# One list of expert tiles for both batches, in two parts, and the outputs summed one tile in every slot

## The reference

```python
x = x + xattn(layernorm(x), ctx, ctx, mask, W_out)       # 16 heads of 32, 128 keys
x = x + ffn(layernorm(x), proj_w, anchors, temp, w1, w2)
# ffn: logits from tanh(x @ proj_w.T / 0.3) against six anchor vectors;
# the two best of 6 experts by softmax of their two logits;
# h = gelu(x @ w1[e])   (512 -> 256);  y = h @ w2[e]   (256 -> 512)
# out = sum over the two chosen experts of weight * y
```

## Time and profile before

| | |
|---|---|
| median of 3 runs | 720.03 us (714.55 to 720.48) |
| the profiled execution | 721.91 us |
| its span, first to last instruction | 720.2 us |
| PE busy | 617.0 us (86%) |
| DVE, ACT, POOL busy | 451.5, 341.8, 301.0 us |
| mean granted TensorE clock | 0.918 |
| DMA | 126.25 MB, mean 175 GB/s |

### The profile page before, as it was taken

The page is one execution under the profiler, slowest core; times in us unless marked ns, Lnnn a source line. Parts: engine busy times, 40 slices in busy tenths (PEclk is TensorE's granted clock), DMA queues, the critical chain, the costliest instruction groups (busy, mean ns, idle before and its releaser), DMA issues.

```text
span 720.2 us, 15169 instructions
## 1 busy us (share of the span) xinstructions
PE 617.0 (86%) x4628; PEld 467.8 (65%) x4629; DVE 451.5 (63%) x968; ACT 341.8 (47%) x646; POOL 301.0 (42%) x434
## 2 busy tenths in 40 slices
PE   5989999999999999988788999999999999996000
PEld 4765566666656656444568898998999888885000
DVE  4846756665685866444986555684555676666455
ACT  4536855666847655574844554433333333331000
POOL 5423755555456656557671314130002233222774
PEclk9759999999999999899987999999999999999555
DMA  5301213222212373347372656485787788886787
GB/s 187 93 30 46 88 63 101 76 87 75 88 59 101 108 271 129 133 172 263 132 263 88 208 174 239 149 273 203 263 293 244 256 268 285 295 277 220 226 246 243
DMA packets 62577, 126.25 MB, mean 175 GB/s; under 512 B 7974, under 2 KB 11046, under 8 KB 62508
## 3 DMA queue, kind: packets, MB, share of 16 engines
q1 hardware_dynamic: 52268, 91.80, 37.7%
q0 software_dynamic: 10240, 33.56, 14.5%
HBM read 69.24 MB, written 56.10 MB: 174 GB/s over the span
## 4 chain that ended last, share of the span: by engine, by line
PE 55%; DVE 14%; issue 11%; DMA 7%; POOL 5%; SPq 3%; ACT 2%; DVEq 1%; POOLq 0%; ACTq 0%
PE ps L1477 7%; DMA y_d<-ysb 5%; PE ps L1499 4%; PE ps L1635 4%; PE ps L1522 3%; PE ps L1687 3%; PE ps L1524 3%; PE ps L1688 3%; PE ps L1523 3%; PE ps L1689 3%; PE ps L1711 3%; PE ps L1713 3%; PE ps L1673 3%; PE ps L1712 3%; PE ps L1590 3%
## 5 line engine op out<-in xcount | busy, mean ns | idle before, releaser
L802 POOL DMA_INDIRECT yg<-y_d,sidx x64 | 64.1, 1002 | 170.4 <-DVE wst L1320 133.9
L1078 DVE TENSOR_REDUCE nmax<-ps 128x4 f32<-128x512 f32 x128 | 82.3, 686 | 45.6 <-PE ps L1477 45.4
L917 ACT ACTIVATE prob<-ps 128x512 f32<-128x512 f32 x128 | 66.1, 603 | 84.2 <-PE ps L1502 81.4
L729 POOL DMA_INDIRECT xs_d<-x,place_now x64 | 67.2, 1049 | 81.0 <-PE ps L1689 66.8
L1687 PE MATMUL ps<-w1H,xgH 128*128 x296 | 90.5, 306 | 2.9 <-DVE xgL L1344 2.9
L1688 PE MATMUL ps<-w1H,xgL 128*128 x296 | 83.9, 283 | 0.0
L1689 PE MATMUL ps<-w1L,xgH 128*128 x296 | 83.8, 283 | 0.0
L996 ACT ACTIVATE xgH<-ps 128x512 fp32r<-128x512 f32 x74 | 44.2, 597 | 80.9 <-PE ps L1673 68.7
L1477 PEld LDWEIGHTS ps<-kfT,qT 32*128 32x128 f32 x1024 | 69.6, 202 | 18.9 <-issue 16.3
L1477 PE MATMUL ps<-kfT,qT 32*128 32x128 f32 x1024 | 76.9, 295 | 1.9 <-DVE nmax L1078 1.4
L1357 DVE COPY ysb<-ps 128x512 f32<-128x512 f32 x74 | 51.0, 689 | 31.4 <-PE ps L1713 19.6
(11 more groups left out here) (195 smaller groups left out, 1373.2 us busy)
## 6 DMA issues: line engine op xcount, KB each, us to landing
xg<-xs_d SPq DMA_DIRECT2D x74, 256.0 KB
y_d<-ysb SPq DMA_DIRECT2D x74, 256.0 KB
xin<-in_x SPq DMA_DIRECT2D x32, 256.0 KB, 2.7
x<-in_x SPq DMA_DIRECT2D x32, 256.0 KB
x_d<-x SPq DMA_DIRECT2D x32, 256.0 KB
x2t<-x_d SPq DMA_DIRECT2D x16, 256.0 KB, 4.1
x2c<-x_d SPq DMA_DIRECT2D x16, 256.0 KB, 4.7
out_x<-x2c SPq DMA_DIRECT2D x16, 256.0 KB
```

What stands on the lines that cost most here:

```text
L729: nc.gpsimd.indirect_dma_start(xs_d, bass.IndirectOffsetOnAxis(ap=place_now[:, n % 2, k, t:t + 1], axis=0), x2[:, n % 4, t, :], None).then ...
L802: nc.gpsimd.indirect_dma_start(yg[:, k, z, :], None, y_d[b], bass.IndirectOffsetOnAxis(ap=sidx[:, k, z:z + 1], axis=0))\
L917: nc.scalar.activation(prob[v % 2][:, h, :], ps[:, B_SC + h, :], ACT.Exp, scale=scale).then_inc(exp_done, 1)
L1078: nc.vector.tensor_reduce(nmax[:, n % 2, :, g * hpg + h], ps[:, token_bank(v, h), :].rearrange("p (t k) -> p t k", t=4), axis=AX.X, op=ALU ...
```

## The change

The expert regions hold both batches: region e has room for 4096 rows, and tokens of blocks 0 to 7 are placed one behind the other. There is one sequence of 69 tiles, the most that 8192 rows over 6 experts can need. The first 27 (T1) are full tiles of the rows of blocks 0 to 3 (4096 rows fill at least 27), so they need no zeros; the other 42 are ordered by the blocks after which a tile is full: those that blocks 0 to 3 fill first, then those that block 4 fills, and so on (`tiles_of_classes`, `first_of_classes`). So the results of blocks 0 to 3 are all in the first 37 tiles, those of block 4 in 45, of block 5 in 53, of block 6 in 61, of block 7 in 69 (`TILES_OF`).

Each list is made with one entry in each partition (`list_of`, ten small operations) and turned to a row by two PE transposes (`turn_list`), which DVE copies to the tables (`keep_list`). For the first list PE does this in the last but one attention step, and it waits for the copies before the projection of block 7, because bank 0 is used by both. For the second list PE waits in slot 23 until DVE is done with `list_of`, which it does at the end of its slot 22.

Token tile c is summed in slot 46 + c for c = 0 to 27, one in every slot, fetched by POOL two slots earlier; tiles 28 to 31 are done behind the loop. Residuals 0 to 15 are loaded in slots 28 to 43, the others five slots behind the sum whose buffer they take. From tile 26 on ACT copies the result to `ysb`. DVE's sums read `share` directly, without the small copies to `wst` and `sidx`. `SPAN` is 7, all loops are written out, and there is one `fill_up`, in slot 21.

```diff
-    NT = (2 * seq + EXPERTS * (P - 1)) // P
...
+    region = batches * seq + P
+    rows = EXPERTS * region
+    def most_tiles(n):
+        return (2 * n * blk + EXPERTS * (P - 1)) // P
+    T1 = 2 * NB1 * blk // P - (EXPERTS - 1)
+    tiles = most_tiles(nblk)
+    TILES_OF = [most_tiles(max(n + 1, NB1)) for n in range(nblk)]
...
-        SPAN = 8
+        SPAN = 7
...
-        TABLE = SPAN * LATE - 1
+        TABLE = SPAN * (LATE - 1) + 5
...
+        ONE_Y, BY_ACT = 20, 26
+        def expert_loop(body):
+            for i in range(n_iter):
                 body(i)
...
+        def put_slot(c):
+            s = TILES_OF[0] + 9 + c
+            return s if s < SLOTS and TILES_OF[c // 4] < tiles else None
...
@@ sync @@
-                if s == S_END - 1:
-                    fill_up(0)
...
+                    if TPI * i + k == TABLE + 2:
+                        fill_up()
...
+                        if w == T1:
+                            scattered_all(nblk)
+                            sp.wait_ge(pad_zero, 16 * EXPERTS)
...
+                    c = TPI * i + k - T1 - 1
+                    if live(c, RX):
+                        load_residual(c)
+                    for c in puts(TPI * i + k - 2):
+                        store_out(c)
+                    for c in puts(TPI * i + k - 5):
+                        if c + RX < ntok:
+                            load_residual(c + RX)
...
@@ gpsimd @@
+            def fetch_outputs(c):
+                pool.wait_ge(yrow_done, c // 4 + 1)
+                after(pool, cmb_done, c - RY + 1)
                 for z in range(2):
+                    nc.gpsimd.indirect_dma_start(yg[:, c % RY, z, :], None, y_d[0:TILES_OF[c // 4] * P, :],
+                                                 bass.IndirectOffsetOnAxis(ap=y_row[:, c, z:z + 1], axis=0))\
+                        .then_inc(yg_in[c % RY], 16)
...
+                    for c in puts(TPI * i + k + 2):
+                        pool.wait_ge(zp_ready, nblk)
+                        pool.wait_ge(up_ready, min(TPI * i + k - L_UP + 1, tiles))
+                        landed(c)
+                        fetch_outputs(c)
...
@@ scalar @@
+                    w, p, n = tl(i, k, L_DN)
+                    if live(w, tiles) and w >= BY_ACT:
+                        act.wait_ge(y_ready, w + 1)
+                        after(act, y_out[p], 16 * n)
+                        nc.scalar.activation(ysb[:, p, :], ps[:, y_bank(w, p), :], ACT.Copy).then_inc(ya_done, 1)
...
@@ vector @@
+            def put_together(c):
+                x = x2t[:, c % RX, :]
+                dve.wait_ge(x2t_in[c % RD], 16 * (c // RD + 1))
+                dve.wait_ge(yg_in[c % RY], 32 * (c // RY + 1))
+                nc.vector.scalar_tensor_tensor(x, yg[:, c % RY, 0, :], share[:, c, 0:1], x, ALU.mult, ALU.add).then_inc(half_done, 1)
+                dve.wait_ge(half_done, c + 1)
+                nc.vector.scalar_tensor_tensor(x, yg[:, c % RY, 1, :], share[:, c, 1:2], x, ALU.mult, ALU.add).then_inc(cmb_done, 1)
...
+                    if TPI * i + k == TABLE:
+                        tiles_of_classes()
+                    if TPI * i + k == TABLE + 2:
+                        first_of_classes()
+                    if TPI * i + k == TABLE + 3:
+                        list_of(CLASSES, nblk)
                         dve.wait_ge(share_done, nblk)
+                    if TPI * i + k == TABLE + 4:
+                        keep_list(B_LATE, T1, T2)
+                        rows_to_tiles()
+                    rows_of_tokens(TPI * i + k - TABLE - 5)
+                    for c in puts(TPI * i + k):
+                        put_together(c)
...
@@ tensor @@
+            def turn_list(bank, count):
+                pe.wait_ge(lst_done, count)
+                for z in range(2):
+                    last = nc.tensor.transpose(ps[0:1, bank, z * P:(z + 1) * P], lst[:, z:z + 1], ident[:])
+                last.then_inc(lst_turned, 1)
...
+            pe.wait_ge(tab_done, 2)
             for t in range(4):
                 project(INSIDE, t)
-            pe.wait_ge(tab_done, 3)
...
+                    if TPI * i + k == TABLE + 4:
+                        pe.wait_ge(used_done, nblk)
+                        turn_list(B_LATE, 2)
```

More of the change, by code:

```diff
@@ L80, in xattn_moe @@
     x2_d = dram("x2_d", [nblk, 4, P, emb], F32)
-    xs_d = dram("xs_d", [batches * rows, emb], F32)
+    xs_d = dram("xs_d", [rows, emb], F32)
     x2_rows = x2_d.rearrange("n t p d -> (n t) p d")
-    y_d = [dram(f"y{b}_d", [NT * P, emb], F32) for b in range(batches)]
+    y_d = dram("y_d", [tiles * P, emb], F32)
     ctx = ExitStack()
@@ L231, in xattn_moe @@
         cursor[0] = spare
[L233 to L247, removed]
+        cnt = sb("cnt", [P, CLASSES, EXPERTS])
+        ntil = sb("ntil", [P, CLASSES + 1, EXPERTS])
+        nbef = sb("nbef", [P, CLASSES + 1, EXPERTS, EXPERTS])
+        nto = sb("nto", [P, CLASSES + 1, EXPERTS])
+        nall = sb("nall", [P, CLASSES + 1])
+        nleft = sb("nleft", [P, CLASSES])
+        whole = sb("whole", [P, EXPERTS])
+        first = sb("first", [P, CLASSES, EXPERTS])
+        zero_row = sb("zero_row", [P, CLASSES, EXPERTS])
+        row_step = sb("row_step", [P, SEGS])
+        begun = sb("begun", [P, SEGS])
+        prod = sb("prod", [P, SEGS])
+        lrow = sb("lrow", [P, 1])
+        lexpert = sb("lexpert", [P, 1])
+        lst = sb("lst", [P, 2])
+        zero_row1 = sb("zero_row1", [P, EXPERTS])
+        bound = sb("bound", [P, EXPERTS, CLASSES + 1])
+        moveby = sb("moveby", [P, EXPERTS, CLASSES + 1])
+        change = sb("change", [P, EXPERTS * (CLASSES + 1)])
+        within = sb("within", [P, 2 * 4, EXPERTS * (CLASSES + 1)])
+        moved = sb("moved", [P, 2 * 4])
         assert cursor[0] <= nc.sbuf_usable_end
@@ L434, in tl, with y_moved, puts @@
             return w, (k - lag) % places, (TPI // places) * i + (k - lag) // places
[L436 to L452, removed]
-        def y_bank(w, p):
-            return B_Y if isinstance(w, int) and w < ONE_Y else B_Y + p
-        def expert_loop(eng, body):
-            for i in range(LEAD):
-                body(i)
[L461 to L478, removed]
+        ONE_Y, BY_ACT = 20, 26
+        assert TABLE + 4 < TPI * (T1 // TPI) and L_DN + ONE_Y > TABLE + 4
+        def y_bank(w, p):
+            return B_Y if w < ONE_Y else B_Y + p
+        def y_moved(eng, count):
+            after(eng, yc_done, min(count, BY_ACT))
+            after(eng, ya_done, count - BY_ACT)
+        def expert_loop(body):
+            for i in range(n_iter):
+                body(i)
+        SLOTS = TPI * n_iter
+        def put_slot(c):
+            s = TILES_OF[0] + 9 + c
+            return s if s < SLOTS and TILES_OF[c // 4] < tiles else None
+        def puts(s):
+            return [c for c in range(ntok) if put_slot(c) == s]
         N_SETUP_LOADS = 4
@@ L505, in store_rows, with fill_up @@
                     sp.dma_start(x2_d[n, t, :, :], x2[:, n % 4, t, :]).then_inc(x2_out[n % 2], 16)
[L507 to L514, removed]
+            row_regs = [sp.alloc_register(f"row{k}") for k in range(TPI)]
+            pad_regs = [sp.alloc_register(f"pad{k}") for k in range(EXPERTS)]
+            def fill_up():
+                sp.wait_ge(pad_ready, 1)
+                sp.wait_ge(s_zero, 1)
+                sp.load(pad_regs, tab_pad[0:1, :])
                 for e in range(EXPERTS):
-                    row = sp.snap(row_regs[e], min_val=0, max_val=batches * rows - P)
-                    sp.dma_start(xs_d[bass.ds(row, P), :], zeros[:]).then_inc(pad_zero[b], 16)
+                    row = sp.snap(pad_regs[e], min_val=0, max_val=rows - P)
+                    sp.dma_start(xs_d[bass.ds(row, P), :], zeros[:]).then_inc(pad_zero, 16)
             def load_w1(e):
@@ L626, in experts @@
[L626 to L634, removed]
-                        sp.dma_start(x2c[:, q, :], x2_rows[CPI * j + q, :, :]).then_inc(x2c_in[q], 16)
@@ L652, in _ @@
+            expert_loop(experts)
+            left = [c for c in range(ntok) if put_slot(c) is None or put_slot(c) + 2 >= SLOTS]
+            for c in left:
+                store_out(c)
+            for c in range(RD):
+                sp.wait_ge(o_out[c], 16 * (ntok // RD))
         @block.gpsimd
@@ new lines, in rows_of_tokens @@
+            def rows_of_tokens(n):
+                if live(n, nblk):
+                    mine = place[:, 4 * n:4 * n + 4, :].rearrange("p t k -> p (t k)")
+                    each = [P, 2 * 4, EXPERTS * (CLASSES + 1)]
+                    tabled(nc.vector.tensor_tensor(within[:], mine.unsqueeze(2).to_broadcast(each),
+                                                   bound[:].rearrange("p e c -> p (e c)").unsqueeze(1).to_broadcast(each), ALU.is_ge))
+                    tabled(nc.vector.tensor_tensor(within[:], within[:], change[:].unsqueeze(1).to_broadcast(each), ALU.mult))
+                    tabled(nc.vector.tensor_reduce(moved[:], within[:], axis=AX.X, op=ALU.add))
```

(7 more changed lines are left out.)

397 lines of the change are left out of this document (174 added, 223 removed).

## The result

The changed kernel takes 675.7 us (median of four runs, 675.09 to 677.31) against 719.83 beside it (714.55 to 720.48): a ratio of 0.9399, 95% interval 0.9356 to 0.9443. The forecast was 695.0 with a range of 677 to 713, so the gain of 44 us is 19 more than forecast, and the range missed it by 1.3. The profiled execution took 677.31, its span 675.6, its mean granted clock 0.94.

What follows compares the result with a forecast made beforehand. PE was taken to bound the expert loop and POOL's gathers the tail, with DMA the bound of slots 46 to 70 after the change. Span 658.5 + 17.4 + 19.2 = 695.1 us, time 695.0, range 677 to 713.

Steps and rivals of the forecast that it cites:

- tile 0 enters: End of attention: list operations and PE's wait for `keep_list` cost net +1.1 us, bounds -1 and +4.
- tile 0 to tile 44: Slots 2 to 45: old losses stay, PE's new wait in slot 23 adds 3.5 us, bounds 2 and 5.
- tile 44 to tile 68: Slots 46 to 70: DMA becomes the bound, 78.7 + 24.6 + 6.9 = 110.2 us, bounds 92.4 and 128.8.
- drain: From the last tile's entry to the first gather behind the loop: 17.4 us, as before.
- tail: Behind the loop: 8 gathers instead of 32, 7 x 1.42 + 9.2 = 19.2 us for 53.2.
- I take 320: Full DMA rate in slots 46 to 70, GB/s: 4.92 us for a slot of six transfers, 4.10 for five.
- its sign: Slots 46 to 70: DMA share above 0.9, 310 to 340 GB/s, PE busy 70 to 75%, clock at 1.00.
- the far bound: Slots 46 to 70: 389 GB/s, the stage's best three microseconds, would give 92.4 us.
- the late routing's loss: First 17 expert slots: 9.1 us lost to late routing and the slow start, left unchanged by the forecast.
- that rival: Clock falls near 1.2 GHz as PE waits on DMA; 22 such slots give a span of 739; chance 0.06.
- The y buffers: Rival: two y buffers hold the slots; landing up to 11 us, 5.9 a slot, span 721.6; chance 0.08.
- DMA is no limit: Rival: slots 46 to 70 stay within 3.7 us, tile 68 enters at 637, span 673.7; chance 0.06.

Runs made afterwards that it cites:

- one_more_store: Changed kernel with one more 0.262 MB store from SP in each of slots 46 to 69: 692.4 us, ratio 0.9585.
- no_late_residuals: Changed kernel without the residual loads of token tiles 16 to 31 (16 transfers fewer in slots 51 to 66): 669.61 us.
- the repeats: Both kernels profiled once more with no edit: before 721.11 us, changed 677.35 us, ratio 0.9415.
- turn_late: Changed kernel with PE's turn of the late (second) list moved from the start of slot 23 to its end: 674.13 us, ratio 0.9367.
- four_y_buffers: Changed kernel with four buffers for the y copies instead of two: 679.05 us, ratio 0.9424.
- before_two_more: Kernel before the change with two more 0.262 MB stores in each of slots 44 to 75: 738.17 us against 724.87, ratio 1.0216.
- half_behind_gated: Changed kernel with token tiles 16 to 31 summed behind the loop, POOL first waiting there for all y stores: 704.87 us, ratio 0.9738.
- all_three: Changed kernel with late turn of the second list, four y buffers and the zero stores spread over six slots: 678.13 us, ratio 0.9387.

## Why the prediction was wrong

The place of the gain and what becomes the bound were right; the size of one term was not, and the others miss by up to 5.7 us but cancel to 0.2. Its steps against the first profile of the changed kernel:

| step | forecast, us | measured | off by |
|---|---|---|---|
| tile 0 enters | 380.5 | 374.86 | -5.7 |
| tile 0 to tile 44 | 167.8 | 172.5 | +4.7 |
| tile 44 to tile 68 | 110.2 | 90.86 | -19.3 |
| drain | 17.4 | 19.3 | +1.9 |
| tail | 19.2 | 18.1 | -1.1 |
| span | 695.1 | 675.6 | -19.5 |

**The failed step: "I take 320", the full DMA rate.** The forecast divided rate by busy share, 271 / 0.81 and 296 / 0.90, and took off 4%. The runs put 401 GB/s in its place (406 with more to move). At 401 the 132 transfers of slots 46 to 69 take 132 x 0.262 MB / 401 GB/s = 86 us; the measured 90.86 are 5 more, since the first slots ask for less than DMA could move. The count of transfers was right but for slots 46 and 47, which have four and not five, as no output is ready yet. The mechanism was right too, as one_more_store and no_late_residuals show from both sides, but weaker than forecast: the share was above 0.9 as its sign asked, while the rate was 376 GB/s for 310 to 340 and PE was busy for 95% for 70 to 75%. Rate over share is no capacity here, for the rate rises faster than the share: 0.81 went with 271, 0.90 with 296, 0.91 with 303, but 1.02 with 389 and 1.04 with 401. The row that had the value was at hand: 400 at 1.04 over four microseconds. The forecast used it to deny 453 and 358, but not when it chose the rate; 389 over three microseconds, which served as the far bound, was below what the kernel then held for 40. With 400 the forecast's own sum gives 16 x 3.93 + 6 x 3.47 + 6.9 = 90.6 for that stretch, since slots of five transfers become PE's, and a span of 675.5. That this meets 675.6 is in part luck, for the other steps cancel, and slot by slot it went otherwise: slots 51 to 55, with six transfers each, still took 3.54 us, while 389 GB/s moved 26 of their 30 transfers, and slots 66 to 69, which ask for 19, took 3.99 us each and moved 23.

**Tile 0's entry.** DVE's list operations and PE's wait for `keep_list` are there (PE waits 2.76 us at 357.83, for DVE's `tab_col`). The 5.7 us are not theirs: identical work up to this point was seen to end anywhere in 373.02 to 383.85. A term of 1 us cannot be told in it. (The forecast's working has a slip of 0.3 us here: 7 x 0.4 + 11 x 0.23 is 5.3, not 5.0.) By the forecast's own sign, a start of the experts that moves by more than 4 us, it was also wrong here; the spread shows that this sign could not tell anything.

**Slots 2 to 45.** The forecast left the late routing's loss at 9.1 us in fewer slots; the 17 slots take 71.9 us instead of 68.1, 3.8 more, of which 1.2 comes back in the next three (10.4 for 11.6). PE's wait in slot 23 came where it was forecast, with 3.46 us from the copy to the next tile's entry, the two transposes included, for 3.5; but 2.2 us of lateness ahead of it and 2.3 of lower clock behind it made tiles 20 to 23 8.1 us longer than before. From slot 25 on 2.5 us came back in this profile (71.7 for 74.2), and 0.9 between the repeats (72.8 for 73.7). Two things make that up. In the kernel before, tile 32 enters 1.4 us late (0.8 in its repeat), because DVE's y copy at 503.21 waits 2.71 us for a y store, behind the six DMAs of `fill_up`; the forecast left this price in these slots, and it is gone from them. The other 1.1 us are PE's pace in this one profile, 3.41 us a slot for 3.47 in the repeat and before (turn_late has 3.41 too); why the pace differs stays open.

**Drain and tail.** The tail is within 1.1 us of the forecast. The drain was 19.3 here and 17.0 in the repeat.

**The rivals.** The clock stayed at 1.00 over the whole stretch from tile 44 to tile 68, with PE busy in 95% of it rather than the 71% forecast, so the condition of that rival never arose; with one_more_store PE was busy for 56.05 of 69.34 us, 81%, and the clock was 1.00 too. It did fall in slot 23, behind 5.3 us of idle time. The y buffers are refuted as the bound by four_y_buffers, which gained 1.8 us. "DMA is no limit" is false as a mechanism, by one_more_store and no_late_residuals, though its time, 673.7 for the span, is nearer to the measured one than the forecast's. The Trainium skill's 358 GB/s (DMA: Bandwidth & Descriptors, "Where 436 GB/s comes from") would by estimate have given 99 us for the stretch, nearer than the forecast's 110; as a ceiling no run bears it out, for 401 were held over 40 us and 406 over 69.

## What to carry to other kernels

Bracket a DMA limit. The highest rate of any window whose share is above 1, however short, is the fast end: 400 here, where 401 to 406 were held in one kernel but 367 in before_two_more. Rate over share of a stage that is not full is the slow end: 335, below both. Here the slow end, taken for the value, made a stretch 21% too long; in before_two_more the fast end would have made a slot 11% too short. Then count the transfers of each slot and compare with what PE alone would take, slot by slot. Work moved out of a tail into slots costs only the excess over that: here 35 us of tail (53.2 - 18.1) were bought for 7.6 us of longer slots (90.86 - 24 x 3.47); for 12 of the token tiles alone, 32.2 us for 7.4 (half_behind_gated). A wait that stands out in such a stretch (12 waits for y stores, 28.9 us) may be only how a full queue shows; doubling the buffer tells, in one run.

## What the runs showed of the hardware

- One core alone moved 401 to 406 GB/s over 40 to 69 us, reads, writes and gathers mixed, at a share of 1.04 to 1.05; another mix held 367 over 86 us at a share of 1.02, and 362 at 1.00 went with a PE that hardly waited.
- Idle time of 5.3 us on PE took the clock to 0.50 for some 6 us, at a price of 2.3 us; with PE busy for 81% of 69 us, its gaps at most 1.5 us, it stayed at 1.00. In before_two_more one gap of 2.40 us was followed by 0.53 and 0.61 over the next 4 us, another of 2.27 us by 1.00.
- The part ahead of the expert loop ended at 373.0 to 383.9 us in executions with the same work.
- The gelu of slot 22 was 3.5 us late in both profiles of the changed kernel, released by "remote"; neither spreading SP's burst nor moving PE's code changed it. In all_three three engines stood together one slot later instead.
